# A two-layer transformer kernel: the second layer's queries and keys are projected with features on partitions and brought to the attention layout by DMA alone

## The chip, the cores and the metric

The kernel runs on one core of a Trainium2 chip. The metric is the device time of one execution in microseconds (us). TensorE is written PE, its weight loads PEld, VectorE DVE, ScalarE ACT, GpSimd POOL, and SyncE, which only issues DMAs here, SP.

## The reference

The input x has 2 x 1024 tokens of 256 features. Two layers follow, each of the form x + attention(layernorm(x)) + ffn(layernorm(x)):

```python
xn = _layernorm(x)
x = x + _L0_attn_ref(xn, ...) + _L0_ffn_ref(xn, ...)   # 32 heads of 8, 8 key heads, causal; gelu, float8
xn = _layernorm(x)
x = x + _L1_attn_ref(xn, ...) + _L1_ffn_ref(xn, ...)

def _L1_attn_ref(x, wq, wk, wv, wo, inv_freq):          # 16 heads of 16
    q = apply_rope((x @ wq.T).reshape(b, s, H, HD), inv_freq)
    k = apply_rope((x @ wk.T).reshape(b, s, H, HD), inv_freq)
    v = (x @ wv.T).reshape(b, s, H, HD)
    scores = jnp.einsum('bshd,bstd->bsht', q, k) / jnp.sqrt(jnp.float32(HD))   # over the heads of one token
    weights = jax.nn.softmax(scores, axis=-1)
    attn = jnp.einsum('bsht,bstd->bshd', weights, v)
    return attn.reshape(b, s, HIDDEN) @ wo.T

def apply_rope(x, inv_freq):        # x1, x2 are the even and the odd features of a head
    return jnp.concatenate([x1 * cos - x2 * sin, x1 * sin + x2 * cos], axis=-1)
```

The second layer's attention is within a token: the 16 heads of a token attend to each other. A tile of 128 tokens is therefore 128 little problems of 16 x 16. Eight tokens are put side by side (8 x 16 = 128 rows), and an indicator in 8 more rows of the operands subtracts a huge number where two rows are of different tokens.

## The kernel before

The 2048 tokens are 16 tiles of 128. Every step of the kernel is a stage, a Python function such as `qkv1`, `gT` or `vw`, and `stage.n` is the stage for tile n (or part n of it). Each engine has a list of stages in `ORDER`, written out by hand as one string per engine, and runs them strictly in that order; semaphores alone tie the engines together. So on every engine a stage that waits holds all that stand behind it. SP's list is the order in which nearly all DMAs are issued, and they go through one queue.

PE's heavy work in the first layer is `qk.Q` (scores of one pair of key block and half of the heads, L692) and `pv.Q` (their product with the values, L706), 144 of each, with ACT's `exp.Q` (L958) between them; `up`, `down` are the first feed-forward (L743, L757), `gu` and `dn1` the second (L875, L885). `xnT`, `obT`, `attT`, `o1T`, `at1T` are transposes on PE. Results of PE go to three shared PSUM banks psA, psB, psC in turn; a stage waits until the engine named in `EMPTIED` has taken what stood in its bank.

For tile n of the second layer the stages around the change are:

- `xs.n` (DVE) splits the normalised tile in two float16 parts, `xt.n` (SP, L548) turns them by DMA into xhs, features on partitions.
- `qkv1.2n` (PE, L782) gives queries and keys of 128 tokens by 512 features in six matmuls of 512 columns (xhs stationary), `qkv1.2n+1` the values in six of 256.
- `qk1c.n` (ACT, L991) copies queries and keys out of PSUM. `ro1.n` (DVE, L1400, L1401) and `ro1p.n` (POOL, L1674, L1676) multiply by cos and sin, `ro2.n` (DVE, L1407, L1409) adds and subtracts into rqkv; `v1c.n` (DVE) puts the values there.
- `vw.n` (SP, L501) writes queries, keys and values to qkvscr in HBM, `vr.n` (SP, L509) reads them back in three DMAs, with a row for each head of each of eight tokens and 16 groups side by side, in runs of 64 bytes. For even tiles they land in G, for odd ones in spare halves of w8g and w8l.
- `gT.2n` and `gT.2n+1` (PE, L795) transpose the queries and the keys, four transposes each; `gTq.n` (DVE, L1416) and `gTk.n` (ACT, L1007) copy them to qk1T (odd tiles: in kTf).
- `S1.n` (PE, L828) makes the scores, 16 matmuls with 24 rows, `ex1.n` (ACT, L1016) the exponentials, `PV1.n` (PE, L839), `o1r.n`, `o1T.n`, `o1.n` the outputs, `ow.n` and `at1r.n` (SP, L514, L520) bring them through HBM to one row for each token, `at1T.n`, `wo1.n`, `yo.n`, `yout.n`, `out.n` finish the tile. `hx`, `ht.n` (SP, L556) and `dn1.n` are the feed-forward's end.

At the start `load_first`, `load_constants` and `load_rest` are called ahead of SP's list, with `wt.0`, `wg.0`, `wg.1`, `wt.1` (raw weights) between them. A second pass over all tiles with safer arithmetic exists in the program and isn't taken in these runs.

Of the kernel before, what the change touches and what calls it, by code (L numbers as in the profile page):

```python
# [6 lines left out]
ALU = mybir.AluOpType  # L7
# [181 lines left out]
         "hh": 2, "ge4": 2}  # L189

QUAD_STAGES = {"pe": ("qk", "pv"), "act": ("exp",), "pool": ("mask",)}

# [1576 lines left out]
```

## Time and profile before

| | |
|---|---|
| three runs | 564.24, 564.69, 565.04 us, median 564.69 |
| the profiled execution | 564.45 us, span of its profile 562.7 us |
| PE, ACT, DVE, POOL busy | 518.6, 468.0, 391.0, 234.7 us |
| DMA | 46.05 MB in 214,396 packets |

The span is the time from the first to the last instruction that the profiler saw; 1.75 us of the execution lie outside it. "Busy" is the time in which an engine had at least one instruction running. A row of the grouped view names line, engine, operation, output and inputs, count, then busy time and mean duration of one, then the engine's idle time ahead of them with what ended it.

### The profile page before, as it was taken

To read this page: it belongs to the slowest core of one execution; us is meant where nothing else is said; L and a number is where in the kernel's file an instruction comes from. 1 tells how busy PE (TensorE), PEld (TensorE's weight loads), DVE (VectorE), ACT (ScalarE), POOL (GpSimd) and SP (SyncE) were. 2 spreads that over 40 slices of the span, in tenths; PEclk is the share of its full clock that TensorE was granted. 3 is DMA by queue.
4 is the path that set the end of the run, shared out by engine and by line. 5 is a ranking of instruction groups with operands and counts; after the bars stand their busy time and mean duration, and the time that the engine had idled before them with its cause. 6 is when DMAs were issued, how large, how long until landed. Compare 5 with 4: busy or idle time off the path is not lost.

```text
span 562.7 us, 12411 instructions
## 1 busy us (share of the span) xinstructions
PE 518.6 (92%) x4661; PEld 256.9 (46%) x4705; DVE 391.0 (69%) x845; ACT 468.0 (83%) x607; POOL 234.7 (42%) x302
## 2 busy tenths in 40 slices
...
GB/s 272 284 62 99 57 24 11 73 40 40 47 91 48 103 36 94 62 76 29 77 51 45 128 49 79 85 82 96 75 90 66 53 85 66 68 70 132 125 105 94
DMA packets 214396, 46.05 MB, mean 82 GB/s; under 512 B 197440, under 2 KB 213056, under 8 KB 214336
## 3 DMA queue, kind: packets, MB, share of 16 engines
q1 hardware_dynamic: 213760, 44.93, 40.5%
q8 instruction: 37, 0.61, 0.5%
q10 hardware_dynamic: 576, 0.33, 0.4%
...
## 4 chain that ended last, share of the span: by engine, by line
PE 77%; DMA 6%; DVE 4%; ACT 4%; SPq 3%; issue 3%; POOL 2%; DVEq 0%; ACTq 0%
PE psV L706 23%; PE psS L692 8%; PE psA L875 3%; PE psC L782 3%; PE psS L828 3%; PE psC L875 3%; ACT Pt L958 2%; PE psB L875 2%; PE psB L885 2%; PE psA L885 2%; PE psB L839 2%; PE psA L782 2%; PE psA L743 2%; PE psB L743 2%; PE psC L743 1%
## 5 line engine op out<-in xcount | busy, mean ns | idle before, releaser
L958 ACT ACTIVATE Pt<-psS 128x1024 f32<-128x1024 f32 x288 | 280.1, 1031 | 24.0 <-PE psS L692 19.2
L706 PE MATMUL psV<-Pt,vaug 128*32 128x512 f32 x1152 | 149.8, 605 | 1.8 <-POOL Pt L1633 1.4
L1633 POOL TENSOR_SCALAR_AFFINE_SELECT Pt<-Pt 128x1024 f32<-128x1024 f32 x64 | 71.6, 1143 | 75.7 <-ACT Pt L958 75.5
L692 PE MATMUL psS<-qTf,kTf 32*128 32x512 f16 x576 | 65.8, 388 | 4.8 <-ACT Pt L958 3.1
L692 PEld LDWEIGHTS psS<-qTf,kTf 32*128 32x128 f16 x576 | 17.9, 91 | 84.2 <-ACT Pt L958 51.4
L1683 POOL TENSOR_TENSOR ss<-ss,mhalf 128x1 f32<-128x1 f32 x16 | 9.6, 597 | 87.0 <-DVE ss L1470 87.0
L706 PEld LDWEIGHTS psV<-Pt,vaug 128*32 128x32 f32 x1152 | 25.4, 108 | 42.7 <-issue 34.7
L1016 ACT ACTIVATE stage<-psS 128x1024 f32<-128x1024 f32 x32 | 31.0, 1023 | 7.0 <-PE psS L828 6.9
L1624 POOL TENSOR_TENSOR QXf<-rt,QXf 128x512 f16<-128x512 f32 x16 | 19.9, 1242 | 27.4 <-ACT QXf L945 27.4
L1304 DVE SCALAR_TENSOR_TENSOR gw<-gw,gb 128x512 f32<-128x512 f32 x32 | 27.6, 866 | 4.8 <-ACT gw L973 4.8
L1613 POOL TENSOR_TENSOR rt<-qkv,cs 128x320 f32<-128x320 f32 x16 | 16.1, 1003 | 27.4 <-DVE qkv L1189 19.8
L875 PE MATMUL psA<-wguT,xhs 128*128 128x512 bf16 x97 | 25.4, 380 | 0.9 <-issue 0.5
L1032 ACT ACTIVATE qtmp<-qtmp 128x1024 bf16<-128x1024 f32 x16 | 17.0, 1063 | 10.9 <-DMA stmp<-qtmp 7.8
L1476 DVE SCALAR_TENSOR_TENSOR qtmp<-qtmp,ss 128x1024 f16<-128x1024 f32 x16 | 21.5, 1344 | 6.3 <-ACT qtmp L1037 6.2
L1313 DVE SCALAR_TENSOR_TENSOR ga<-gw,gb 128x512 bf16<-128x512 f32 x32 | 23.0, 718 | 2.0 <-ACT gw L984 2.0
L1674 POOL TENSOR_TENSOR r<-qk,cos 128x256 f32<-128x256 f32 x16 | 13.4, 835 | 25.8 <-ACT qk L991 18.9
L984 ACT ACTIVATE gw<-gw 128x512 f32<-128x512 f32 x32 | 20.8, 651 | 0.0
L1616 POOL TENSOR_TENSOR rt<-qkv,sn 128x160 f32<-128x160 f32 x32 | 20.8, 669 | 0.0
L973 ACT ACTIVATE gw<-gb 128x512 f32<-128x512 bf16 x32 | 20.7, 649 | 0.1
L1455 DVE SCALAR_TENSOR_TENSOR stmp<-stmp,psA 128x512 f32<-128x512 f32 x17 | 11.6, 684 | 12.4 <-ACT stmp L1026 12.2
L1037 ACT ACTIVATE qtmp<-qtmp,ss 128x1024 f16<-128x1024 f32 x16 | 18.5, 1156 | 1.2 <-POOL ss L1683 1.2
L782 PE MATMUL psC<-wqkv,xhs 128*128 128x256 f16 (+1 forms) x102 | 19.1, 324 | 0.0
...
## 6 DMA issues: line engine op xcount, KB each, us to landing
...
```

Of the source, the lines that this page charges most:

```text
L692: e.matmul(psS[j], kd[32 * j:32 * j + k, h, 128 * at:128 * at + 128], qd[32 * j:32 * j + k, 4 * h:4 * h + 4, :].rearrange("p s n -> p (s n ...
L706: ins = e.matmul(psV[32 * j:32 * j + 32, :], vaug[:, at, j, 32 * h:32 * h + 32], Pt[(4 * Q + j) % NP], start=(kb == 0 and h == 0), stop=(k ...
L743: ins = e.matmul(bank[:, 128 * k:128 * k + 128], wt8[:, c, c0:c0 + 128], src[:, c, :], start=(c == 0), stop=(c == 1))
L782: ins = e.matmul(bank[:, 0:c1 - c0], src[:, pt, 128 * a:128 * a + 128], wparts[:, q, a, c0:c1], start=(k == 0), stop=(k == 5))
L875: ins = e.matmul(bank[:], src[:, pt, 128 * c:128 * c + 128], wguT[:, c, c0:c0 + 512], start=(k == 0), stop=(k == 3))
L885: ins = e.matmul(bank[:, 0:256], hT[:, pt, s, :], wpT[:, s, :], start=(k == 0), stop=(k == 15))
L958: e.activation(flat(Pt4[:, u % NP:u % NP + 2, :]), flat(psS4[:, j:j + 2, :]), ACT.Exp, scale=scale).then_inc(S["exp"], 1)
L1016: e.activation(P1[:, 4 * b:4 * b + 8, :].rearrange("p g n -> p (g n)"), flat(psS4[:, b:b + 2, :]), ACT.Exp, scale=SC1).then_inc(S["ex1"], 1)
L1304: e.scalar_tensor_tensor(gw[:, half, :], gw[:, half, :], 1.0 / GA, gb[:, half, :], ALU.add, ALU.mult).then_inc(S["ge1"], 1)
L1313: e.scalar_tensor_tensor(a, gw[:, half, :], 1.0, gg, ALU.add, ALU.mult).then_inc(S["ge3"], 1)
L1476: e.scalar_tensor_tensor(hx_b[:, 1, :], h1, sn[:, 2:3], hx_b[:, 0, :], ALU.mult, ALU.subtract).then_inc(S["hx"], 1)
L1633: e.affine_select(out=p, in_=p, pattern=[[0, 8], [1, 128]], compare_op=ALU.is_ge, fill=0.0, base=0, channel_multiplier=-1).then_inc(S["mas ...
```

## The change

Queries and keys are now projected with features on partitions: the weights are stationary, 128 features at a time, and the 128 tokens move. `qkv1.2n` is 24 matmuls of 128 columns where it was six of 512; the columns of the weights are reordered on the host so that partition p = 16d + h holds feature pair d of head h (`turn`), first all even features, then all odd ones. The tables of cos and sin get the same layout (`turns`, 128 partitions by 1024 tokens); they are made once, by two more activations in `sin.0`, four stages `tT` of four transposes each on PE and five stages `tTc` on ACT. `rab.n` (DVE) multiplies by them straight from PSUM in two instructions of 512 elements, `rr.n` (POOL) adds and subtracts in two of 256, writing the heads that belong to one group side by side. `rw.n` (SP) writes them to rscr in two DMAs, in runs of 8 floats (32 bytes); `rd.n` (SP) reads them in four DMAs of 16 partitions, in runs of 512 bytes, right to where `gTq` and `gTk` had put them. The stages `gT`, `gTq`, `gTk`, `qk1c`, `ro1`, `ro1p`, `ro2` are gone from the first pass. The values alone go through vscr (`vw.n`, one DMA of 128 KB in runs of 64 bytes; `vr.n`, one where there were three), and `at1r.n` reads runs of 64 bytes where it read rows of 1 KB. The first loads become stages in SP's list, two raw weights (`wgx`) and the later tiles of x (`lx`) are issued by ACT, and the casts `w8` no longer wait for a buffer between the second and the third. All lists in `ORDER` are written anew, so every stage may stand elsewhere.

```diff
+                    if part == 0:
+                        for c in range(4):
+                            for k, (pt, q, a) in enumerate(((0, 0, 0), (1, 0, 0), (0, 1, 0), (0, 0, 1), (1, 0, 1), (0, 1, 1))):
+                                ins = e.matmul(bank[:, 128 * c:128 * c + 128], wparts[:, q, a, 128 * c:128 * c + 128],
+                                               src[:, pt, 128 * a:128 * a + 128], start=(k == 0), stop=(k == 5))
+                        ins.then_inc(S["qkv1"], 1)
+                        return
...
+            def tT(m):
...
+                    ins = e.transpose(bank[:, 128 * k:128 * k + 128], turns[:, 1 + m // 2, c0:c0 + 128], identf[:])
...
+            def rab(n):
...
+                w.wait_ge("qkv1", 2 * n + 1)
+                w.wait_ge("rr", 2 * n)
+                for k in range(2):
+                    e.tensor_tensor(r1[:, k, :].rearrange("p (e s t) -> p e s t", e=2, s=2), bank,
+                                    turns[:, k:k + 2, t0:t0 + 128].unsqueeze(2).to_broadcast([128, 2, 2, 128]),
+                                    ALU.mult).then_inc(S["rab"], 1)
...
+            def rr(n):
+                dst = flat(rqkv[n % 2][:, 0:2, :])
+                w.wait_ge("rab", 2 * n + 2)
+                w.wait_ge(f"d_rw{n % 2}", 32 * (n // 2))
+                for f, op in enumerate((ALU.subtract, ALU.add)):
+                    e.tensor_tensor(dst[:, 256 * f:256 * f + 256].rearrange("p (b s j a) -> p s b j a", b=4, s=2, j=4),
+                                    by_group(r1[:, f, 0:256]), by_group(r1[:, f, 256:512]), op).then_inc(S["rr"], 1)
...
+            def rw(n):
+                src = flat(rqkv[n % 2][:, 0:2, :]).rearrange("p (f m a) -> p f m a", f=2, a=8)
+                dst = rscr[n].rearrange("b s j (f i) (h a) -> f (i h) (b s j) a", f=2, a=8)
+                for f in range(2):
+                    w.wait_ge("rr", 2 * n + f + 1)
+                    e.dma_start(dst[f], src[:, f, :, :]).then_inc(S[f"d_rw{n % 2}"], 16)
+
+            def rd(n):
+                w.wait_ge(f"d_rw{n % 2}", 32 * (n // 2 + 1))
...
+                w.wait_ge("S1", 4 * (n - 1))
+                for b in range(4):
+                    dst = (qk1Todd if odd(n) else qk1T)[32 * b:32 * b + 16, :, :, :].rearrange("p s j n -> p (s j) n")
+                    e.dma_start(dst, rscr[n, b].rearrange("s j d n -> d (s j) n")).then_inc(S[f"d_rd{n % 2}"], 16)
...
+                e.activation(turns[:, 2, :].rearrange("p (m h) -> p m h", h=16),
+                             ang[:, 0, :].unsqueeze(2).to_broadcast([128, 64, 16]), ACT.Sin)
...
-    "gT": lambda m: ("gTk" if m % 2 else "gTq", m // 2 + 1), "gTagain": lambda n: ("gTm", n - NT + 1),
+    "gT": lambda m: ("gTk" if m % 2 else "gTq", m // 2 - NT + 1), "gTagain": lambda n: ("gTm", n - NT + 1),
```

On PE, from the scores of tile 5 to those of tile 6, this stood in a row before (L795 are the transposes gT, L828 the scores S1, L839 is PV1, L692 qk, L706 pv, L743 up, L875 gu, L610 and L611 xnT):

```order
L828 MATMUL psS<-kTf 128x128 x16
L706 MATMUL psV<-Pt,vaug 32x512 x8
L795 MATMUL psB<-identf,G 128x128 x4
L692 MATMUL psS<-qTf,kTf 128x512 x4
L610 MATMUL psC<-identf,xn 128x128
L611 MATMUL psC<-identf,xn 128x128
L875 MATMUL psA<-wguT,xhs 128x512 x4
L839 MATMUL psB<-stage,w8l 32x128 x16
L692 MATMUL psS<-qTf,kTf 128x512 x4
L743 MATMUL psC<-x8T,w8g 128x128 x8
L795 MATMUL psA<-identf,G 128x128 x4
```

And at the same place now (L842 is the new projection, L903 S1, L764 pv, L801 up, L950 gu, L750 qk, L914 PV1, L785 and L786 wo0):

```order
L842 MATMUL psC<-xhs,wqkv 128x128 x24
L785 MATMUL psA<-wo,attT 128x256
L786 MATMUL psA<-wo,attT 128x256
L903 MATMUL psS<-kTf 128x128 x16
L764 MATMUL psV<-Pt,vaug 32x512 x4
L801 MATMUL psB<-x8T,big 128x128 x8
L950 MATMUL psC<-wguT,xhs 128x512 x4
L750 MATMUL psS<-qTf,kTf 128x512 x4
L950 MATMUL psA<-wguT,xhs 128x512 x4
L764 MATMUL psV<-Pt,vaug 32x512 x4
L750 MATMUL psS<-qTf,kTf 128x512 x4
L764 MATMUL psV<-Pt,vaug 32x512 x4
```

The groups of four transposes are gone from between the first layer's work, and nothing takes their place.

On SP, near the end, from ow.11 on, the list before (L514 ow, L520 at1r, L525 out, L509 vr, L556 ht, L548 xt, L501 vw):

```order
L514 DMA oscr<-o_0 128x16x16
L520 DMA at_0<-oscr 128x256
L525 DMA out<-yout 128x256
L509 DMA w8g<-qkvscr 128x16x16 x2
L509 DMA w8l<-qkvscr 128x16x16
L556 DMA_TRANSPOSE stmp<-qtmp 128x16x128
L548 DMA_TRANSPOSE xhs<-xn1T 128x4x128
L501 DMA qkvscr<-rqkv 128x3x256
L514 DMA oscr<-o_0 128x16x16
L509 DMA G<-qkvscr 128x16x16 x3
```

The list now, from ow.11 on (L573 ow, L565 rd, L579 at1r, L587 out, L557 rw, L524 vw, L618 ht, L610 xt, L537 vr):

```order
L573 DMA o2scr<-o_0 128x256
L565 DMA kTf<-rscr 16x8x128 x4
L579 DMA at_0<-o2scr 128x16x16
L587 DMA out<-yout 128x256
L557 DMA rscr<-rqkv 128x32x8 x2
L524 DMA vscr<-rqkv 128x16x16
L618 DMA_TRANSPOSE stmp<-qtmp 128x16x128
L610 DMA_TRANSPOSE xhs<-xn1T 128x4x128
L537 DMA G3v<-vscr 128x16x16
L573 DMA o2scr<-o_0 128x256
L565 DMA qk1T<-rscr 16x8x128 x4
```

The writes and reads of queries and keys, six issues, stand between the steps of the last tiles; xt.15 comes behind rw.14 and vw.14.

On ACT, at the start, the list before ran tc.0 (L931, L932), qh.0 (L945), sin.0 (L924, L925), wh.0 (L995), g.0 (L966), qh.1 and then exp.0 (L958):

```order
L931 ACT_TABLE_LOAD
L931 ACTIVATE qtmp<-r 128x1024
L932 ACTIVATE qtmp<-r 128x1024
L945 ACTIVATE QXf<-rt 128x32x16
L924 ACT_TABLE_LOAD
L924 ACTIVATE sin<-ang 128x64
L925 ACTIVATE cos<-ang,hpi 128x64
L995 ACTIVATE wqkv<-stmp 128x1536
L966 ACTIVATE gb<-psC 128x512
L945 ACTIVATE QXf<-rt 128x32x16
L958 ACT_TABLE_LOAD
L958 ACTIVATE Pt<-psS 128x1024 x2
```

The list now, from wh.0 on (L1094 wh, L1061 sq, L1019 and L1020 tc, L1033 qh, L1046 exp, L1007 to L1012 sin):

```order
L1094 ACTIVATE wqkv<-stmp 128x1536
L1061 ACTIVATE gw<-gb 128x512
L1019 ACTIVATE qtmp<-r 128x1024
L1020 ACTIVATE qtmp<-r 128x1024
L1033 ACTIVATE QXf<-rt 128x32x16
L1046 ACTIVATE Pt<-psS 128x1024 x4
L1007 ACT_TABLE_LOAD
L1007 ACTIVATE sin<-ang 128x64
L1008 ACTIVATE cos<-ang,hpi 128x64
L1010 ACTIVATE big<-ang 128x1024
L1012 ACTIVATE big<-ang,hpi 128x1024
L1046 ACT_TABLE_LOAD
```

sin.0 now stands behind exp.0 and exp.1, with a table load on either side, and has two new activations of 1024 elements. Ahead of the rows shown, ACT now runs qh.0, g.0, sq.0, fh.0, g.1, fh.1 and th.0; with the sq.1 shown (L1061), six stages of the feed-forward have moved ahead of exp.0.

## Rows read from the trace of the kernel before

**Rows 1.** The page: busy time of each engine, share of the span

```profile
PE 518.6 (92%) x4661; PEld 256.9 (46%) x4705; DVE 391.0 (69%) x845; ACT 468.0 (83%) x607; POOL 234.7 (42%) x302
```

**Rows 2.** Windows: length, PE, PEld, DVE, ACT, POOL busy, clock, DMA share, GB/s

```profile
0.00:20.00 20.00, 5.84 (x16) 2.91 (x16) 13.26 (x38) 3.91 (x4) 5.99 (x19) 1.00 0.94 301
...
40.00:80.00 40.00, 35.04 (x286) 13.82 (x284) 31.27 (x62) 38.72 (x53) 27.65 (x32) 1.00 0.21 55
80.00:120.00 40.00, 36.85 (x283) 15.66 (x285) 35.20 (x72) 38.50 (x53) 22.29 (x28) 1.00 0.22 52
...
160.00:200.00 40.00, 39.74 (x402) 20.69 (x406) 28.09 (x64) 38.81 (x55) 17.42 (x24) 1.00 0.45 72
...
360.00:400.00 40.00, 39.63 (x411) 21.67 (x407) 24.69 (x54) 34.94 (x44) 13.65 (x18) 1.00 0.59 109
...
500.00:520.00 20.00, 17.67 (x188) 11.65 (x189) 14.93 (x35) 7.78 (x11) 4.87 (x8) 1.00 0.59 108
520.00:540.00 20.00, 16.54 (x206) 12.02 (x207) 12.65 (x26) 8.76 (x12) 1.94 (x4) 1.00 0.80 124
540.00:563.00 23.00, 16.23 (x136) 10.55 (x135) 12.30 (x34) 6.07 (x8) 1.04 (x2) 0.85 0.42 93
```

**Rows 3.** The timeline of PE from 404 us: start, duration of the group

```profile
404.75 0.66 PE L795 MATMUL psA<-identf,w8g 128*128 128x128 f32 x4
405.25 0.60 PE L715 MATMUL psB<-identf,ob 128*128 128x128 f32 x4
405.68 1.46 PE L782 MATMUL psC<-wqkv,xhs 128*128 128x512 f16 x6
407.07 0.39 PE L692 MATMUL psS<-qTf,kTf 32*128 32x512 f16 x4
407.40 0.62 PE L743 MATMUL psA<-x8T,w8g 128*128 128x128 fp8e4 x8
407.86 0.61 PE L743 MATMUL psB<-x8T,w8g 128*128 128x128 fp8e4 x8
```

**Rows 4.** Groups by line, shapes apart: busy us, mean ns | idle before

```profile
L782 PEld LDWEIGHTS psC<-wqkv,xhs 128*128 128x128 f16 x102 | 9.2, 98 | 7.4 <-issue 3.0
...
L1674 POOL TENSOR_TENSOR r<-qk,cos 128x256 f32<-128x256 f32 x16 | 13.4, 835 | 25.8 <-ACT qk L991 18.9 <-DVE rqkv L1409 5.8 <-issue 0.9
...
L1464 DVE SCALAR_TENSOR_TENSOR qtmp<-stmp,psA 128x512 f32<-128x512 f32 x10 | 6.8, 682 | 1.7 <-PE psA L875 1.5
...
L991 ACT ACTIVATE qk<-psC 128x512 f32<-128x512 f32 x8 | 4.9, 608 | 1.1 <-PE psC L782 1.1
...
L931 ACT ACTIVATE qtmp<-r 128x1024 bf16<-128x1024 f32 x3 | 3.2, 1074 | 6.6 <-DMA r<-in_wgu 6.2 <-DVE wguT L1150 0.4
```

**Rows 5.** DMA queues, the whole span: packets, MB, share of 16 engines

```profile
q1 hardware_dynamic: 213760, 44.93, 40.5%
```

**Rows 6.** DMA queues from 505 to 508.5 us, where ow.11 writes alone

```profile
q1 hardware_dynamic: 2064, 0.13, 36.5%
```

**Rows 7.** DMA queues from 491.8 to 496.3 us, where vr.12 reads

```profile
q1 hardware_dynamic: 6226, 0.41, 91.8%
```

**Rows 8.** The timeline of SP from 480 us: start and duration of each issue

```profile
504.65 0.36 SPq L514 DMA_DIRECT2D oscr<-o  x1
509.38 0.33 SPq L520 DMA_DIRECT2D at<-oscr  x1
...
515.95 1.19 SPq L548 DMA_TRANSPOSE xhs<-xn1T  x1
...
547.95 0.36 SPq L514 DMA_DIRECT2D oscr<-o  x1
```

**Rows 9.** The chain that ended last, from 0 to 45 us

```profile
19.92 5.71 DMA stage<-in_wg
...
28.20 1.28 ACT L958
29.49 1.94 ACT Pt L958 x2
```

More of the change, by code:

```diff
@@ L225 @@
     "wo0": lambda n: ("xa", n + 1), "up": lambda m: ("fh" if m % 2 else "g", m // 2 + 1), "down": lambda n: ("yff", n + 1), "flagT": lambda n: ("flag", 1), "wsum": lambda m: ("wmin", m + 1),
-    "xn1T": lambda n: ("xn1f", n - NT + 1), "qkv1": lambda m: ("v1c" if m % 2 else "qk1c", m // 2 + 1),
-    "gT": lambda m: ("gTk" if m % 2 else "gTq", m // 2 + 1), "gTagain": lambda n: ("gTm", n - NT + 1),
+    "xn1T": lambda n: ("xn1f", n - NT + 1), "qkv1": lambda m: ("v1c", m // 2 + 1) if m % 2 else ("rab", m + 2) if m < 2 * NT else ("qk1c", m // 2 - NT + 1),
+    "tT": lambda m: ("tTc", m + 1),
+    "gT": lambda m: ("gTk" if m % 2 else "gTq", m // 2 - NT + 1), "gTagain": lambda n: ("gTm", n - NT + 1),
     "PV1": lambda n: ("o1r", n + 1),
@@ L257 @@
 idc vz tab cst w8 w8m w8s tsc tm tcs tw ln0 xn xnTc qkvc va wide q0 kl xs fTc rmax rcomb mxn mTc ob att attTc xa ge1 ge3 ge3b a8c yff
-wh wsq wsum ln1 xn1 xn1Tc xn1f wl wmin v1c ro1 ro2 gTq m1 gTm o1r o1 sg hh ssm hx at1Tc yo yout osum flag rng rngb
+wh wsq wsum ln1 xn1 xn1Tc xn1f wl wmin v1c tT tTc rab rr gTq m1 gTm o1r o1 sg hh ssm hx at1Tc yo yout osum flag rng rngb
 zero gz zf rs0 rope ql mask ge4 xf rs1 ro1p rsg w8a""".split()
@@ L562, in all_landed @@
                     w.wait_ge(f"d_vw{p}", 16 * 8 * passes)
-                w.wait_ge("d_vr", 48 * NT * passes)
+                for p in range(2):
+                    w.wait_ge(f"d_vr{p}", read_back(NT * passes - 2 + p))
+                    w.wait_ge(f"d_rd{p}", 128 + 64 * 8)
                 w.wait_ge("d_ow", 16 * NT * passes)
@@ L809, in S1m @@
             def S1m(n):
-                w.wait_ge("gTq", n + 1)
-                w.wait_ge("gTk", n + 1)
+                w.wait_ge("gTq", n - NT + 1)
+                w.wait_ge("gTk", n - NT + 1)
                 for j in range(4):
@@ L818, in S1m @@
                             ins.then_inc(S["S1m"], 1)
+            def tT(m):
+                w.wait_ge("sin", 1)
+                w.wait_ge("d_id", 16)
+                bank = shared("tT", m)
+                for k in range(4):
+                    c0 = 512 * (m % 2) + 128 * k
+                    ins = e.transpose(bank[:, 128 * k:128 * k + 128], turns[:, 1 + m // 2, c0:c0 + 128], identf[:])
+                ins.then_inc(S["tT"], 1)
             def S1(n):
-                k = 24 if n < NT else 25
-                w.wait_ge("gTq", n + 1)
-                w.wait_ge("gTk", n + 1)
+                if n < NT:
+                    w.wait_ge(f"d_rd{n % 2}", 128 + 64 * (n // 2 + 1))
+                w.wait_ge("gTq", n - NT + 1)
+                w.wait_ge("gTk", n - NT + 1)
                 w.wait_ge("gTm", n - NT + 1)
@@ L987, in qk1c, with tTc @@
                 w.wait_ge("qkv1", 2 * n + 1)
-                w.wait_ge("ro1p", 2 * (n + 1 - len(qk1)))
-                w.wait_ge("ro1", 2 * (n + 1 - len(qk1)))
+                w.wait_ge("ro1p", 2 * (n - NT))
+                w.wait_ge("rab", 2 * n)
                 bank = psM[filled["qkv1", 2 * n] % len(psM)]
-                e.activation(qk1[n % len(qk1)][:], bank[:], ACT.Copy, scale=1.0 / WUP if n < NT else 1.0).then_inc(S["qk1c"], 1)
+                e.activation(qk1[0], bank[:], ACT.Copy).then_inc(S["qk1c"], 1)
+            def tTc(m):
+                if m == 4:
+                    w.wait_ge("tT", 4)
+                    w.wait_ge("tTc", 2)
+                    e.activation(turns[:, 2, :], turns[:, 0, :], ACT.Copy).then_inc(S["tTc"], 1)
+                    return
+                bank = psM[filled["tT", m] % len(psM)]
+                w.wait_ge("tT", m + 1)
+                e.activation(turns[:, m // 2, 512 * (m % 2):512 * (m % 2) + 512], bank[:], ACT.Copy,
+                             scale=1.0 / WUP).then_inc(S["tTc"], 1)
             def wh(n):
@@ L1037, in hxa @@
                 e.activation(hx_b[:, 0, :], h1, ACT.Copy, scale=ss[n % len(ss)][:, 2:3]).then_inc(S["hxa"], 1)
-            run = {"wh": wh, "wsq": wsq, "qh": qh, "g": g, "hxa": hxa, "sin": sin, "tc": tc, "tde": tde, "exp": exp, "sq": sq, "fh": fh, "th": th, "qk1c": qk1c, "gTk": gTk, "ex1": ex1,
+            run = {"tTc": tTc, "wgx": wgx, "lx": lx, "wh": wh, "wsq": wsq, "qh": qh, "g": g, "hxa": hxa, "sin": sin, "tc": tc, "tde": tde, "exp": exp, "sq": sq, "fh": fh, "th": th, "qk1c": qk1c, "gTk": gTk, "ex1": ex1,
                    "tg": tg, "ssq": ssq}
@@ L1387, in v1c @@
                                 ALU.mult).then_inc(S["v1c"], 1)
-            def half1(k, s):
-                return r1[:, k, 256 * s:256 * s + 256].rearrange("p (h d) -> p h d", d=8)
-            def ro1(n):
-                src = qk1[n % len(qk1)][:].rearrange("p (h d e) -> p h d e", d=8, e=2)
-                cb = cos1[:, n % NB, :].unsqueeze(1).to_broadcast([128, 32, 8])
-                sbb = sin1[:, n % NB, :].unsqueeze(1).to_broadcast([128, 32, 8])
-                w.wait_ge("sin", 1)
-                w.wait_ge("tc", 12)
-                w.wait_ge("qk1c", n + 1)
-                w.wait_ge("ro2", 2 * n)
-                e.tensor_tensor(half1(1, 0), src[:, :, :, 0], sbb, ALU.mult).then_inc(S["ro1"], 1)
-                e.tensor_tensor(half1(1, 1), src[:, :, :, 1], cb, ALU.mult).then_inc(S["ro1"], 1)
+            def rab(n):
+                bank = psM[filled["qkv1", 2 * n] % len(psM)][:].rearrange("p (e s t) -> p e s t", e=2, s=2)
+                t0 = 128 * (n % NB)
+                w.wait_ge("tTc", 5)
+                w.wait_ge("tc", 12)
+                w.wait_ge("qkv1", 2 * n + 1)
[4 more added lines that the diff above has]
+                                    ALU.mult).then_inc(S["rab"], 1)
```

243 lines of the change are left out of this document (145 added, 98 removed), and 238 rows, old and new, of the table ORDER.

## The prediction

> **What bounds the kernel now.** First the page: PE is busy 518.6 of 562.7 us, ACT 468.0, DVE 391.0 [rows 1]. A mean over the span doesn't say where a microsecond of PE is worth one, so I read the windows next [rows 2]. They show three stretches. Up to about 120 us ACT is the fuller engine: 38.7 of 40 us and 38.5 of 40, with PE at 35.0 and 36.9. From 160 us PE is at 39.7 of 40 with ACT at 38.8, and by 360 us PE stands alone, 39.6 against 34.9. From 500 us on nothing is full: PE has 17.7 of 20, 16.5 of 20 and 16.2 of 23, while DMA has a share of 0.59 and then 0.80. So there is an ACT stretch, a long PE stretch and a tail of latencies through HBM. Each edit is priced by the stretch in which it lies.
>
> The chain that ended last says the same of the two ends. At the start it goes through loads, 5.7 us for the last raw weights among them, and the first exponential runs at 29.5 us [rows 9]. In the tail SP's timeline shows ow.11 issued at 504.65, at1r.11, which waits for its landing, at 509.38, and xt.15 at 515.95 [rows 8]. I call 504.65 the start of the tail; from there to the span's end are 58.05 us.
>
> **The transposes go.** Four transposes gT take 0.50 us of PE from their start to the next group's (404.75 to 405.25) [rows 3]. A group itself lasts 0.66, and where the next isn't ready part of its end shows too; I take 0.55, between 0.50 and 0.60. Of 32 such groups 26 (tiles 0 to 12) stand ahead of the tail: 14.3 us, with bounds of 13.0 and 15.6. Those of tiles 0 to 4 lie where ACT is nearly as full as PE, so they count only if ACT loses as much. It does: qk1c and gTk are gone, 0.61 us each [rows 4], 1.2 a tile against 1.1 on PE. The six groups in the tail stand where PE idles: 0.
>
> **The projection.** Six matmuls of 512 columns take 1.39 us (405.68 to 407.07). The new one has 24 of 128 columns, each with its own weights. `up` is the same pattern in another type, eight matmuls of 128 columns in 0.46 us (407.40 to 407.86), 57.5 ns each [rows 3]; 24 make 1.38 us, so this costs nothing. Below that it can't go, since the columns are the same number. The upper bound is a weight load that nothing hides: 98 ns each, the mean of the float16 loads of this very projection [rows 4], 24 of them 2.35 us, 0.96 more a tile, 14.4 us for the 15 tiles projected before the tail's middle. I take 0, because `up` also shows loads of 98 ns and keeps the pace of 57.5. The Trainium skill has a rule against this edit: TensorE: Matmul & The Clock Gate, Back-to-back issue gap, gives about 81 ns for each matmul in a sustained stream of loads and matmuls of 128 columns. By that the projection is 1.94 us and the kernel some 8 us slower than by the row; the trace of `up` does not agree with it.
>
> **The rotation.** DVE gives up six instructions (ro1, ro2, gTq) and gets two of 512 elements from PSUM, nearest row 0.68 us each; POOL keeps two of 256 elements, 0.84 [rows 4]. DVE is at 25 to 35 us of 40 all through the middle [rows 2], so its gain is hidden. What is new is that rab reads PSUM itself: the shared bank is held until DVE comes to it, for 1.4 us where ACT took 0.61. PE's other stages need that bank third next; I allow 0 to 4 us and put it with the waits below.
>
> **The start.** ACT's list, in the ACT stretch: four tTc of 512 elements and one of 1024, 3.5 us; two sines of 1024, 2.1; a further table load, 1.28 as ahead of exp.0 [rows 9]: 6.9 us more (1024 elements by L931, 1.07, 512 by L991 [rows 4]). Against it stand qk1c.0 and qk1c.1 (1.2) and six stages of 0.62 us moved ahead of exp.0, where ACT waited for loads (3.8). The loads: the three raw weights that were queued behind constants and x are issued at once on two queues, and the cast of the third no longer waits. But the transposes qt.0 and kt.0 still queue behind some 6 MB, which at the 301 GB/s of the first 20 us [rows 2] takes, with what is issued late, until about 24 us, so the first exponential comes at 26 to 28 us where it was 29.5; I take 2 us of gain. The sum is -0.1: nothing, with bounds of -4 and +4. The four tT on PE, 2.0 us, fall in the ACT stretch, where PE has 3 to 5 us of slack in 40 [rows 2]: 0, at most 2.
>
> **DMA.** Runs set its time. ow.11 alone: 2064 packets in 36.5% of 16 engines over 3.5 us, 9.9 ns a packet of 64 bytes written; vr.12: 6226 in 91.8% over 4.5 us, 10.6 ns a packet read [rows 6, 7]. For a tile, rw writes 8192 packets of 32 bytes. No row has them; between nothing less than half a packet of 64 (5 ns) and the whole queue's mean, 40.5% of 16 x 562.7 over 213,760, 17 ns [rows 5], I take 10, since the 64-byte row is nearest: 5.1 us. rd (512 packets) is about 1 us, at1r has 2048 packets for 128, 0.9 us more, vr loses two of three DMAs of 2048, 2.6 us less. So a tile has some 4.3 us more of DMA, and the queue's share goes from 0.41 to about 0.53. The Trainium skill, DMA: Bandwidth & Descriptors, Specifications, says that transfers under 512 bytes are read-modify-write. Here 64-byte writes cost no more than 64-byte reads; 32-byte ones are not in the trace.
>
> **The middle's latency.** From qkv1 to S1 the new path needs 1.4 + 1.4 (rab) + 1.7 (rr) + 7.5 (rw: 5.1 and the fixed part of a lone DMA, for which I take 2.4: ow.11 took 4.7 [rows 8] with 1.4 of transfer, others less) + 4 (rd) = 16 us. Counting PE's stages between the two in the new list at the durations above, tiles 0 to 12 have 24 to 66 us. That covers it with some queueing. But from 340 to 400 us four to five tiles rotate, where DMA has 0.59 of 40 us already [rows 2]; 4.3 each takes it to about 0.95. I add 1 us of stalls for it and for the banks, bounds 0 and 9.
>
> **The tail.** Set T = 0 at ow.11. at1r.11 lands at 8 instead of 6.8 (its own 2048 packets). dn1.11 and ht.12 follow, then xt.15, behind rw.14 and vw.14 on the queue: landed at about 17.5, where before it was issued at 11.3 (515.95). Then rab, rr, rw.15 (issued at 23, landed at 31), rd.15 (36), vr.15 (41, since SP issues it last), PV1.15, ow.15 at 43.5 instead of 43.3 (547.95) [rows 8], at1r.15 1.3 longer, and the rest as before: 59.5 instead of 58.05. The tail's transposes and copies that are gone pay for most of the longer writes. I take +1.5, bounds -2 and +8.
>
> **The sum** is made against the profiled execution: 562.7 - 14.3 + 0 - 0.1 + 1 + 1.5 = 550.8 of span, and 1.75 outside it: 552.5 us. That execution took 564.45, the median of three is 564.69, so the two count as one. What this measurement can tell from no change is about 0.2%, 1.1 us.
>
> **The rivals.**
>
> *DMA takes the middle too (0.15).* If the queue's load between 340 and 400 us and SP's strict order make kt, qt and xt late, qk waits and the whole list with it. For it speaks the share of 0.95, against it the gaps of 24 us and more. It gives back 5 to 12 us: 558 to 564, by its bounds some of it not faster.
>
> *Short writes cost much more (0.10): slower.* Each ns above 10 for a packet of 32 bytes adds 0.5 us a tile. On the path are the last three tiles and the cluster of five at 340 to 400 us, some 8 tiles, 4 us for each ns once the queue is full. It decides from 13 ns on; at 17, the mean packet, it takes 16 us: 568; at 20, 578. For it speaks that a write of 32 bytes is less than anything that the kernel writes now; against it that 64-byte packets show no cost by bytes at all.
>
> *Loads of weights are not hidden (0.07).* At 98 ns the term is 14.4 us: 567. At the skill page's 81 it is 8 us: 560.5. `up` speaks against both.
>
> *The start gains more (0.12).* If the first exponential comes at 24 us and the new order fills the 8 us in which PE idles between 40 and 120 us, 4 to 9 us more go: 544 to 548.
>
> The forecast itself has 0.56, with a range of its own of 548 to 557. The range over all cases is 543 to 566. Faster: the forecast, the better start and two thirds of the first rival and a third of the third, 0.80; within 0.2%: 0.06; slower: 0.14.
>
> **What the new profile should show.** No rows for gT; the projection at 1.35 to 1.45 us from its start to the next group's; about 21,500 packets a tile in q1 and a share of 0.50 to 0.56; PE above 39 of 40 us from 160 us on; ow.11 issued near 490; first exponential at 26 to 28 us. A q1 share above 0.65 means dear short writes. PE at 37 or less of 40 in the middle with waits of qk on kTf or qTf means the first rival. I am wrong if PE's idle time outside the two ends grows by more than 10 us.

## The result, and the profile after

The changed kernel takes 573.69 us (median of four, 571.2 to 574.46) beside 564.87 for the kernel before on the same chip: a ratio of 1.0159, 95% interval 1.0142 to 1.0176. It is 9 us slower where 12 us less was forecast. The profiled execution took 574.46 us.

The page of the changed kernel, against [rows 1, 5]: busy times, the queue, and of its DMA table the row of rw (median us from issue to landing at the end):

```profile
span 572.7 us, 12792 instructions
PE 521.6 (91%) x4881; PEld 262.4 (46%) x4881; DVE 375.2 (66%) x794; ACT 457.7 (80%) x582; POOL 245.9 (43%) x299
...
q1 hardware_dynamic: 313408, 42.50, 50.1%
...
rscr<-rqkv SPq DMA_DIRECT2D x32, 128.0 KB, 6.5
```

Its windows, with the columns of [rows 2]:

```profile
160.00:200.00 40.00, 38.16 (x404) 19.86 (x397) 25.97 (x56) 35.35 (x48) 16.57 (x20) 0.96 0.66 62
...
320.00:360.00 40.00, 37.01 (x432) 20.27 (x428) 26.88 (x58) 31.69 (x39) 23.83 (x29) 1.00 0.78 76
360.00:400.00 40.00, 37.17 (x392) 20.53 (x392) 18.33 (x40) 30.30 (x38) 12.51 (x16) 0.91 0.55 78
500.00:520.00 20.00, 17.12 (x195) 11.26 (x194) 12.73 (x27) 7.97 (x11) 8.33 (x11) 0.94 0.65 78
520.00:540.00 20.00, 16.41 (x213) 12.06 (x215) 10.11 (x21) 6.77 (x8) 2.64 (x3) 0.89 0.80 102
```

From 320 to 400 us PE has lost nearly 6 of 80 us, and its clock is 0.91 behind 360 us. The window of before that [rows 2] doesn't show:

```profile
320.00:360.00 40.00, 39.64 (x412) 19.85 (x413) 28.80 (x64) 35.77 (x47) 19.75 (x26) 1.00 0.41 67
```

Where the loss comes from is seen in PE's timeline. The first two rows are a projection and what starts behind it, then the start of `qk.96`, the stall, and `qk.102`:

```profile
327.75 1.50 PE L842 MATMUL psC<-xhs,wqkv 128*128 128x128 f16 x24
329.19 0.40 PE L750 MATMUL psS<-qTf,kTf 32*128 32x512 f16 x4
...
346.74 0.49 PE L750 MATMUL psS<-qTf,kTf 32*128 32x512 f16 x4
...
362.83 0.48 PE L668 MATMUL psB<-identf,at 128*128 128x128 f32 x1 [5.82 <-DMA at<-o2scr]
...
376.78 0.64 PE L750 MATMUL psS<-qTf,kTf 32*128 32x512 f16 x4
```

The 24 matmuls take 1.44 us to the next group's start, as forecast. The same two `qk` groups before the change:

```profile
348.70 0.52 PE L692 MATMUL psS<-qTf,kTf 32*128 32x512 f16 x4
...
372.08 0.48 PE L692 MATMUL psS<-qTf,kTf 32*128 32x512 f16 x4
```

At `qk.96` the new kernel is 2.0 us ahead, and six steps later it is 4.7 behind. One wait of 5.82 us lies between, in at1T.5, for the landing of at1r.5. Behind it PE works at the lower of its two clocks (1.2 GHz; the granted clock is 0.50 from 362.8 to 366.3 us). SP's timeline tells why that is late (a row with x4 is four issues):

```profile
341.50 0.55 SPq L537 DMA_DIRECT2D G3v<-vscr  x1
342.42 10.06 SPq L557 DMA_DIRECT2D rscr<-rqkv  x4
352.52 3.38 SPq L573 DMA_DIRECT2D o2scr<-o  x1
356.01 1.27 SPq L602 DMA_TRANSPOSE qTf<-QXf  x1
358.76 0.38 SPq L579 DMA_DIRECT2D at<-o2scr  x1
359.24 2.66 SPq L565 DMA_DIRECT2D kTf<-rscr  x4
```

Issuing is itself held up. The four issues of rw.7 and rw.8 keep SP for 10.06 us, ow.5 stands behind them and needs 3.38 instead of some 0.4, its data land 6.23 us after its start, and only then can at1r.5 be issued. The tail shows the same thing, against [rows 8]:

```profile
510.17 0.43 SPq L573 DMA_DIRECT2D o2scr<-o  x1
...
515.13 2.64 SPq L557 DMA_DIRECT2D rscr<-rqkv  x2
517.81 3.36 SPq L524 DMA_DIRECT2D vscr<-rqkv  x1
521.28 3.15 SPq L618 DMA_TRANSPOSE stmp<-qtmp  x1
524.54 1.20 SPq L610 DMA_TRANSPOSE xhs<-xn1T  x1
```

ow.11 is issued at 510.17, not near 490, and rw.14, vw.14 and ht.12 hold xt.15 until 524.54, though its input was ready at 518.95 (DVE's last write of xn1T).

### The profile page after: what moved, and what is told of

Its sections match the earlier page's. It is cut to its first block, busy times and chain, and to the rows that moved or that the text cites. A ratio compares the mean times of both kernels' runs of the same rounds, so it can differ in the third digit from the quotient of the medians.

```text
span 572.7 us, 12792 instructions
## 1 busy us (share of the span) xinstructions
PE 521.6 (91%) x4881; PEld 262.4 (46%) x4881; DVE 375.2 (66%) x794; ACT 457.7 (80%) x582; POOL 245.9 (43%) x299
## 4 chain that ended last, share of the span: by engine, by line
PE 63%; DMA 10%; SPq 10%; ACT 6%; DVE 5%; issue 3%; POOL 3%; DVEq 0%; POOLq 0%; ACTq 0%
PE psV L764 18%; PE psS L750 7%; ACT Pt L1046 3%; SPq L557 3%; DMA rscr<-rqkv 3%; PE psB L950 3%; PE psC L950 2%; PE psA L960 2%; PE psS L903 2%; SPq L565 2%; DMA kTf<-rscr 2%; PE psA L950 2%; PE psA L801 2%; DMA stage<-in_wg 1%; POOL rqkv L1782 1%
## 5 line engine op out<-in xcount | busy, mean ns | idle before, releaser
L1046 ACT ACTIVATE Pt<-psS 128x1024 f32<-128x1024 f32 x288 | 279.5, 1030 | 35.8 <-PE psS L750 30.8
L764 PE MATMUL psV<-Pt,vaug 128*32 128x512 f32 x1152 | 153.2, 614 | 1.2 <-POOL Pt L1736 1.1
L750 PE MATMUL psS<-qTf,kTf 32*128 32x512 f16 x576 | 66.6, 391 | 8.7 <-ACT Pt L1046 4.0
L750 PEld LDWEIGHTS psS<-qTf,kTf 32*128 32x128 f16 x576 | 17.9, 91 | 86.0 <-ACT Pt L1046 44.1
L1114 ACT ACTIVATE stage<-psS 128x1024 f32<-128x1024 f32 x32 | 31.0, 1024 | 23.0 <-PE psS L903 23.0
L1782 POOL TENSOR_TENSOR rqkv<-r 128x256 f32<-128x256 f32 x32 | 37.1, 1184 | 24.0 <-DVE r L1494 24.0
L764 PEld LDWEIGHTS psV<-Pt,vaug 128*32 128x32 f32 x1152 | 25.0, 109 | 41.3 <-issue 35.4
L1578 DVE SCALAR_TENSOR_TENSOR qtmp<-qtmp,ss 128x1024 f16<-128x1024 f32 x16 | 22.8, 1423 | 6.4 <-ACT qtmp L1135 6.3
L950 PE MATMUL psB<-wguT,xhs 128*128 128x512 bf16 x92 | 23.7, 380 | 0.0
L950 PE MATMUL psA<-wguT,xhs 128*128 128x512 bf16 x84 | 22.5, 392 | 0.0
L950 PE MATMUL psC<-wguT,xhs 128*128 128x512 bf16 x80 | 20.6, 380 | 0.0
L1061 ACT ACTIVATE gw<-gb 128x512 f32<-128x512 bf16 x32 | 20.5, 645 | 0.1
```

Source lines behind the costliest of these rows:

```text
L750: e.matmul(psS[j], kd[32 * j:32 * j + k, h, 128 * at:128 * at + 128], qd[32 * j:32 * j + k, 4 * h:4 * h + 4, :].rearrange("p s n -> p (s n ...
L764: ins = e.matmul(psV[32 * j:32 * j + 32, :], vaug[:, at, j, 32 * h:32 * h + 32], Pt[(4 * Q + j) % NP], start=(kb == 0 and h == 0), stop=(k ...
L950: ins = e.matmul(bank[:], src[:, pt, 128 * c:128 * c + 128], wguT[:, c, c0:c0 + 512], start=(k == 0), stop=(k == 3))
L1046: e.activation(flat(Pt4[:, u % NP:u % NP + 2, :]), flat(psS4[:, j:j + 2, :]), ACT.Exp, scale=scale).then_inc(S["exp"], 1)
L1061: e.activation(gw[:, half, :], gb[:, half, :], ACT.Square).then_inc(S["sq"], 1)
L1114: e.activation(P1[:, 4 * b:4 * b + 8, :].rearrange("p g n -> p (g n)"), flat(psS4[:, b:b + 2, :]), ACT.Exp, scale=SC1).then_inc(S["ex1"], 1)
```

## The experiments

**One entry of SP's list moved.** rw.8 goes behind at1r.5:

```diff
- rw.7 rw.8 ow.5 qt.13 at1r.5 rd.7 vr.7
+ rw.7 ow.5 qt.13 at1r.5 rw.8 rd.7 vr.7
```

> The changed kernel with one entry of SP's list moved: rw.8, the write of tile 8's queries and keys, goes from ahead of ow.5 to behind at1r.5. Theory (SP's queue in its fixed order): the 5.8 us wait of TensorE at 362.83 us is ow.5 held behind the four blocked issues of rw.7 and rw.8, 10.06 us long; without rw.8's two issues ow.5 goes out about 5 to 6.5 us earlier, the wait falls to under 1 us, the clock is not dropped behind it, and the time falls by 6 to 8 us, to about 566 to 568. Rival (the transfers themselves are the bound, the DMA engines being full of short packets in this stretch): ow.5 lands no earlier than before or the wait comes back at S1 of tile 8, whose rd.8 is later, and the time falls by less than 2 us.

573.25 us, ratio to before 1.0150 (1.0130 to 1.0169): hardly anything, which is the rival's number. SP and PE there:

```profile
350.46 0.34 SPq L573 DMA_DIRECT2D o2scr<-o  x1
...
353.09 0.38 SPq L579 DMA_DIRECT2D at<-o2scr  x1
353.52 4.27 SPq L557 DMA_DIRECT2D rscr<-rqkv  x2
357.89 4.47 SPq L565 DMA_DIRECT2D kTf<-rscr  x4
```

```profile
365.03 1.24 PE L903 MATMUL psS<-kTf 24*128 24x128 f32 x16 [4.57 <-DMA kTf<-rscr]
```

The wait for at1r.5 is gone as the theory has it, but rw.8 now stood ahead of rd.7, and S1.7 waits 4.57 us for that. The move cured one victim and made another. It didn't decide between the theories.

**Long runs.** rw writes the same bytes in rows of 1 KB; the scratch then holds them in another layout, so the second layer's scores are of other features.

```diff
- dst = rscr[n].rearrange("b s j (f i) (h a) -> f (i h) (b s j) a", f=2, a=8)
+ dst = rscr[n].rearrange("b s j d n -> (b s j d n)").rearrange("(f p c) -> f p c", f=2, p=128)
```

> The changed kernel with rw's 256 KB a tile written in rows of 1 KB instead of runs of 32 bytes; everything else, the order included, stays. The scratch then holds the numbers in another layout, so the scores of the second layer are formed from other features and the output is not the reference's. Theory (the price of the short runs is the issues that block SP, not the DMA engines' time): rw's issues fall from 2 to 3.4 us to below 0.5 us each, the wait at 362.83 us falls to under 1 us, the tail's ow.11 goes out nearer 495 us, and the time falls by 10 to 14 us, to 560 to 564. Rival A (the order of the list is the price whatever the packets are): the time falls by less than 4 us. Rival B (the short packets also slow every other transfer): queue q1's share falls from 50.1% by more than 8 points and the time falls by more than 14 us, below 560.

553.85 us, ratio 0.9814 (0.9795 to 0.9832): 11 us below the kernel before and some 20 below the changed one. Page and windows:

```profile
q1 hardware_dynamic: 186432, 42.50, 38.7%
...
rscr<-rqkv SPq DMA_DIRECT2D x32, 128.0 KB, 1.8
```

```profile
320.00:360.00 40.00, 39.79 (x454) 21.50 (x454) 26.52 (x59) 33.95 (x43) 21.84 (x26) 1.00 0.54 99
360.00:400.00 40.00, 39.79 (x417) 20.88 (x412) 20.95 (x46) 35.26 (x45) 15.94 (x20) 1.00 0.55 81
```

Nothing else of the change was touched, so the length of the runs is what turned the gain into a loss. Rival A is out. The share falls by 11.4 points and the time by more than 14 us, which are rival B's numbers: there is more to the short runs than the issues that I had seen blocked. From the starts of the `qk` groups the 21.6 us of span split in 3.0 at 182 us (S1.1 waiting for rd.1), 8.0 between `qk.96` and `qk.102`, 0.9 behind that, and 9.8 from `qk.138` to the end (87.95 us against 78.19; before the change 82.84). Of the 8.0 us PE idles for 5.7, and for 2.3 it takes longer over the same stages, at a mean granted clock of 0.89 where the long runs have 1.00.

**rng.0 behind at1Tc.15** on DVE:

```diff
- yo.14 hx.15 rng.0 at1Tc.15
+ yo.14 hx.15 at1Tc.15 rng.0
```

> The changed kernel with rng.0, the first of the final sampling steps, moved on VectorE behind at1Tc.15, the last copy that the last output projection waits for. Theory: rng.0 lies on the chain of the end (561.54 to 563.69 us), and the time falls by 1.5 to 2.4 us. Rival: the transfer of the last at tile bounds the copy, rng.0 only fills a wait, and the time changes by less than 0.5 us.

575.16 us, 1.0191 (1.0171 to 1.0211): not faster. wo1.15 starts 1.2 us earlier (0.6 of that is there at wo1.14 already), but then the flag's transposition waits 2.16 us for rng, and the last group starts at 566.32 instead of 565.41. rng.0 is on the end's path on either side of the copy.

**The suspected cost alone, in the kernel before.** Ahead of each vw.n, SP writes 256 KB of the same tile to a scratch that nobody reads, in 8192 runs of 32 bytes; and as a control the same bytes by the same two issues in rows of 1 KB.

```diff
+ def xw(n):
+     w.wait_ge("ro2", 2 * n + 2)
+     for f in range(2):
+         e.dma_start(dst[f], src[:, f, :, :]).then_inc(S[f"d_xw{n % 2}"], 16)
```

> The kernel before with one thing added: ahead of each of its sixteen vw.n SP also writes 256 KB from the same tile to a scratch that nobody reads, in 8192 runs of 32 bytes, by two issues, as rw does in the changed kernel. Nothing else of the change is in. Theory (blocked issues of short runs in SP's fixed order cost time by themselves): queue q1's share rises by 8 to 11 points, each added pair holds SP 2.5 to 6 us, and the kernel gets 5 to 15 us slower, to 570 to 580, mostly at waits for ow and at1r that follow an added pair and in the tail. Rival (the cost is in the changed kernel's own order or in its rd reads, which this kernel has not): below 3 us slower.

> The control to the extra short runs: the kernel before with the same added 256 KB a tile, by the same two issues at the same places of SP's list, but in rows of 1 KB (256 packets a tile). With short runs it took 73 us more. Theory (the short packets are the price): under 8 us more than before. Rival (any two issues and 256 KB more at that place cost as much): over 30 us more.

Short: 637.84 us, 1.1313 (1.1283 to 1.1342), 73 us more. Long: 568.29 us, 1.0079 (1.0060 to 1.0099), 4.4 more. SP around one such pair, first with the short runs (then vw, at1r):

```profile
190.58 2.50 SPq L510 DMA_DIRECT2D xscr<-rqkv  x2
193.13 3.35 SPq L503 DMA_DIRECT2D qkvscr<-rqkv  x1
196.52 1.15 SPq L529 DMA_DIRECT2D at<-oscr  x1
```

and with the long ones:

```profile
181.93 0.82 SPq L510 DMA_DIRECT2D xscr<-rqkv  x2
182.79 0.45 SPq L503 DMA_DIRECT2D qkvscr<-rqkv  x1
183.28 0.53 SPq L529 DMA_DIRECT2D at<-oscr  x1
```

The pair holds SP for 2.5 us, and the next write is held for 3.35 more. vw now lands after 6.5 us (median) where it took 2.7. PE then waits in many places: 5.18 and 5.17 us for at at 200 and 405 us, 4.28 and 5.37 for G at 150 and 481. Of the 73 us PE idles for 48, and for 25 it takes longer over the same work (busy 543.7 us where it was 518.6), at a mean granted clock of 0.93 where it was 0.98. I had expected 5 to 15 us and was far too low. The reason is probably that a list that was laid out for vw landing in 2.7 us has no room for 4 more anywhere; no run shows that by itself. The changed kernel, with lists laid out anew, pays 20 us instead of 73.

**Half of each rw from another queue.** ScalarE issues the second half, at the place of its list where the addition is done; bytes, runs and DMA engines stay.

```diff
  def rw(n):                            # SP
-     for f in range(2):
-         w.wait_ge("rr", 2 * n + f + 1)
-         e.dma_start(dst[f], src[:, f, :, :])...
+     w.wait_ge("rr", 2 * n + 1)
+     e.dma_start(dst[0], src[:, 0, :, :])...
+ def rwa(n):                           # ACT
+     w.wait_ge("rr", 2 * n + 2)
+     e.dma_start(dst[1], src[:, 1, :, :])...
```

> The changed kernel with the second of rw's two issues (features 8 to 15 of every head, 4096 runs of 32 bytes) taken from SP and given to ScalarE's queue, behind the addition that makes it; the bytes, the runs and the 16 DMA engines stay the same, and SP keeps the first issue, which took 0.36 to 0.44 us where it was not held up. Theory A (the price of the short runs is SP's blocked second issue and what queues up behind it): SP's part of each rw falls from 2.5 to 3.5 us to about 0.5 us, the wait at 362.83 us shrinks to under 1.5 us and the tail loses about 5 us, so the time falls by 10 to 16 us, to 558 to 564. Theory B (the transfers are the price: the engines are full of 8192 short packets whoever issues them, and rd or ow lands late anyway): less than 4 us is won. ScalarE pays for its issues too: if they block it for 2 us each, it gets slower than the changed kernel.

566.54 us, 1.0053 (1.0029 to 1.0078): about 6 us less than the changed kernel by the ratios, between the two theories. ScalarE's timeline, then SP's and PE's in the tail:

```profile
338.58 0.41 ACTq L1009 DMA_DIRECT2D rscr<-rqkv  x1
...
339.87 4.33 ACTq L1009 DMA_DIRECT2D rscr<-rqkv  x1
```

```profile
500.51 3.62 SPq L588 DMA_DIRECT2D out<-yout  x1
504.17 0.54 SPq L574 DMA_DIRECT2D o2scr<-o  x1
```

```profile
512.59 0.48 PE L669 MATMUL psB<-identf,at 128*128 128x128 f32 x1 [4.54 <-DMA at<-o2scr]
```

A lone issue of 4096 short packets takes 0.36 to 0.58 us on either queue; the one that follows 1.3 us after another is held for 4.33 us. So it is what is still outstanding on the issuer's own queue that holds it: SP's issue for rw.8, at 338.5 us right behind that for rw.7, is held for 3.15 us, and ScalarE's first, 0.1 us later, takes 0.41. ScalarE pays for being held: its next exponential starts at 344.30 us, 2.57 after the end of the one before, and PE waits 1.34 us for it. The wait at 182 us is gone and the one at 363 us is 1.74 us. But in the tail out.9 is held all the same, ow.11 goes out at 504.17 us where the long runs have 496.26, and it lands after 5.4 us where they take 1.7. The DMA share is 1.01 from 500 to 520 us. With two queues the packets' times overlap (the share is 1.11 from 320 to 360 us), so this number doesn't say how full the 16 engines are.

**The same with xt.15 ahead of ht.12.**

> The kernel with half of rw on ScalarE's queue, and xt.15 ahead of ht.12 in SP's list. In the changed kernel xn1T of tile 15 was ready at 518.95 us and xt.15 was issued at 524.54, behind vw.14 and ht.12; the projection of tile 15 waited 3.26 us for it. Theory (SP's order in the tail costs by itself): 1.5 to 3 us less than with half of rw on ScalarE alone. Rival (once the issues no longer block, the order is no matter): within 1 us of it.

567.44 us, 1.0060 (1.0039 to 1.0082): the rival. PE's wait for xhs (0.81 us) is gone, and the one of S1.14 grows from 0.73 to 2.00 us.

**The lists bent round the short runs**, half of rw still on ScalarE's queue:

```diff
- rw.7 rw.8 ow.5 qt.13 at1r.5 rd.7 vr.7
+ rw.7 ow.5 qt.13 at1r.5 rd.7 vr.7 rw.8
...
- out.9 ow.11 rd.13 at1r.11
+ ow.11 at1r.11 out.9 rd.13
```

> Short runs kept, half of each rw on ScalarE's queue, and the lists bent round them: rw.8 behind rd.7 and vr.7 on both queues, ow.11 and at1r.11 ahead of out.9, xt.15 ahead of ht.12, rd.15 ahead of ht.13, the second half of rw.14 later on ScalarE. Theory (most of what was left, 12 us against long runs, is bad places in the order): 558 to 563 us. Rival (the engines' time for 8192 short packets is what is left, whatever the order): less than 3 us below the kernel with half on ScalarE's queue, 564 to 568.

563.19 us, 0.9947 (0.9927 to 0.9967): by the ratios 6 us less than with half of rw on ScalarE alone. That is the theory's side, at the edge of its range. The profiled execution was one of 567.39. Windows:

```profile
320.00:360.00 40.00, 40.00 (x464) 21.78 (x462) 27.34 (x62) 33.96 (x43) 21.91 (x26) 1.00 0.75 92
360.00:400.00 40.00, 40.00 (x407) 20.18 (x405) 20.95 (x46) 35.27 (x45) 15.09 (x19) 1.00 0.63 87
...
500.00:520.00 20.00, 14.03 (x169) 10.53 (x166) 9.33 (x22) 5.87 (x8) 1.62 (x4) 0.83 1.01 115
```

This parts the cost. In the middle the DMA engines carry the short packets at a share of 0.75 and PE is full: `qk.96` to `qk.102` takes 22.04 us as with long runs, and at `qk.138` the short packets have cost 1.3 us where they cost 11.9. So there the price was the held issues and their places in the list. In the tail no order that I tried helped: from `qk.138` to the end it takes 91.4 us in this execution, at a granted clock of 0.83 from 500 to 540 us. A median execution is 4.2 us shorter, and no trace says where.

**Long runs that end in the layout the second layer needs, first form.** The tokens of a group are put side by side on the way into PSUM, rw writes runs of 256 bytes, and S1 reads its operands at a stride of eight numbers:

```diff
- return turned(n, s)[32 * b:32 * b + 24, j, :]
+ return tile[32 * b:32 * b + 24, :].rearrange("p (n m) -> p m n", m=8)[:, 4 * s + j, :]
```

> A version meant to keep the changed kernel's gain without its short runs, with the right output: the eight tokens of a group are put next to each other on the way (the transposition into PSUM of the rotation tables and the projection write their columns in that order), so that a partition's row for one block is 256 contiguous bytes. rw then writes 1024 runs of 256 bytes a tile instead of 8192 of 32, rd reads 64 rows of 4 KB, and S1 takes its two operands from the tile at a stride of eight numbers instead of one. Order, issues and bytes stay. Theory (the runs' length is the price, 19 us of it): 552 to 557 us, 8 to 12 us below the kernel before. Rival A (S1's operands at a stride cost TensorE: 512 matmuls and their loads, 10 to 20 ns more each): 5 to 10 us more than that, 558 to 566. Rival B (writing PSUM in runs of 16 bytes slows the projection or the rotation behind it): the projection's six matmuls of a quarter take more than 0.38 us.

568.18 us, 1.0052 (1.0033 to 1.0072). Rival B is out, since the projection takes 1.34 to 1.45 us as in the changed kernel. It is rival A, and more than it: groups of S1's weight loads and matmuls here, then the same in the kernel with rows of 1 KB, where the operands are contiguous:

```profile
L908 PEld LDWEIGHTS psS<-kTf 24*128 24x128 f32 x256 | 16.1, 327 | 4.0 <-issue 2.5 <-DMA kTf<-rscr 1.4
L908 PE MATMUL psS<-kTf 24*128 24x128 f32 x256 | 18.4, 435 | 1.0 <-DMA kTf<-rscr 1.0
```

```profile
L903 PEld LDWEIGHTS psS<-kTf 24*128 24x128 f32 x256 | 8.0, 186 | 4.4 <-issue 2.5 <-DMA kTf<-rscr 1.8
L903 PE MATMUL psS<-kTf 24*128 24x128 f32 x256 | 9.5, 283 | 1.4 <-DMA kTf<-rscr 1.4
```

S1 takes 2.28 us a tile instead of 1.17, 17.7 us over sixteen; the distance to the 553.85 of long runs is 14.3. From 120 to 540 us no wait of PE is longer than 0.6 us.

**Second form.** The rotation writes as in the changed kernel, rw in runs of 256 bytes, S1 reads the queries in runs of eight, and DVE copies the keys once to where they stand in a row:

```diff
+ def k1(n):
+     w.wait_ge(f"d_rd{n % 2}", 128 + 64 * (n // 2 + 1))
+     w.wait_ge("S1", 4 * n)
+     for i in range(2):
+         e.tensor_copy(k1c[i].rearrange("p j (h a) -> p j h a", a=8), by_m(n)[:, 4 + 2 * i:6 + 2 * i, :, :])...
```

> Long runs again, and the output is the reference's, but without the stride of eight that made S1 slow: the rotation writes its tile as in the changed kernel, rw writes 1024 runs of 256 bytes a tile, rd reads 64 rows of 4 KB with queries and keys of a head side by side, S1 reads the queries in runs of eight numbers as its moving operand, and VectorE copies the keys once (two copies of 128x256 a tile) into a tile where they stand one after another for the weight load. Theory (run length is the price; eight numbers in a row are read at full speed; the copies of some 0.4 us each are hidden in VectorE's slack of a third): S1 takes 1.2 us a tile again and the kernel 553 to 559 us, 6 to 11 us below the kernel before. Rival (the copy sits on the way from rd to S1 and stands in VectorE's fixed order): 560 to 566. If S1 takes 1.7 us a tile, the moving operand alone is slowed by its runs.

558.64 us, 0.9875 (0.9855 to 0.9896): 7 us below the kernel before, 16 below the changed one by the ratios. S1 takes about 1.1 us again, and PE is full in the middle:

```profile
534.06 0.73 PE L910 MATMUL psS<-kTf 24*128 24x128 f32 x16 [1.97 <-DVE ang L1542]
534.61 0.62 PE L910 MATMUL psS<-kTf,ang 24*128 24x128 f32 x16
```

```profile
320.00:360.00 40.00, 40.00 (x472) 22.14 (x472) 29.57 (x67) 34.06 (x43) 24.07 (x29) 1.00 0.56 92
```

The copy costs waits of 1.2 to 2.0 us at four of the sixteen S1, two ahead of 240 us and two in the tail, the last above.

## Why the prediction was wrong

**What held.** The projection's 24 matmuls take 1.34 to 1.45 us, 56 to 60 ns each (but for the last tile, 2.25 us at the lower clock); 57.5 was the term. The Trainium skill's 81 ns (TensorE: Matmul & The Clock Gate, Back-to-back issue gap) is not what this trace shows. The first exponential comes at 26.5 us, first `qk` 2.4 us earlier, 2 was the term. The packet's price held too: the queue's busy time differs by (0.501 x 572.7 - 0.387 x 551.1) x 16 = 1178 us between short and long runs, for 126,976 packets, 9.3 ns a packet; with the rows of 1 KB that stand in their place it is a little more, near the 10 that I took. In the records the 32-byte packets themselves last 8.1 ns in the mean; the others last longer beside them (those of 64 bytes 11.8 ns, with long runs 10.1). A read-modify-write below 512 bytes, which the Trainium skill states (DMA: Bandwidth & Descriptors, Specifications), doesn't show in a packet's time here. The share is 0.501, the bottom of the range given, 3.7 us a tile and not 4.3. One reason is a term that the text left out: ow now writes rows of 1 KB, so a tile has 19,588 packets and not 21,500. So the rival "short writes cost much more", which was to decide from 13 ns a packet on, is not what happened. (By its own 4 us for each ns, 20 ns would make 580, not 578.)

**What held by luck.** Take the short runs out and the measured 553.85 stands beside the forecast 552.5, but two errors cancel in that. With long runs ow.11 goes out at 496.3 us, 8.4 us earlier than before the change, where transposes and start together were put at 14.4 and ow.11 "near 490". And from there to the end it takes 54.9 us, 3.2 less than before, where 1.5 more was forecast. The transposes themselves were priced rightly: from `qk.42` to PV1.11 the 23 groups that stood there took 11.8 us, 0.51 each. But this stretch is only 7.1 us shorter. One group of pv and one of PV1 more stand in it now, 1.9 us; the other 2.8 are spread over the groups that stayed, and their cause is open. Up to `qk.42` no more than the start's gain is there (1.6 us at `qk.0`, 1.2 at `qk.42`).

**The step that failed** is "The middle's latency". It added up the path from qkv1 to S1, found 16 us against gaps of 24 to 66, and took 1 us of stalls. (One term of the path was too low: POOL's two instructions take 1.18 us each where 0.84 was taken.) At 182 us the path itself was late: S1.1 waited for rd.1, 3.0 us of the price. But nothing on it was late at 363 us, where most was lost. What was late is ow.5, which has nothing to do with it and stands behind rw.7 and rw.8 in SP's list. The text priced rw as 5.1 us of the engines and never as time of the queue that issues it: 2.5 us and more for a pair, 10.06 for two, and up to 3.4 for the plain DMA right behind it. Measured, the term is 11.9 us (3.0 + 8.0 + 0.9) where 1 was taken and 9 was the bound. Over the whole stretch the DMA queue was not full. The text feared a share of 0.95 between 340 and 400 us, for which it took the 0.59 of the window from 360 us for all 60 us; measured are 0.78 up to 360 us and 0.55 behind. The rival "DMA takes the middle too" named SP's strict order and PE at 37 of 40, which is what the windows show; it looked for the waits at kTf and qTf and gave 5 to 12 us back, which for the middle is right. The sign named for being wrong, 10 us more of idle PE outside the ends, didn't come: from 120 us to ow.11 PE idles 8.9 us where it was 3.5. Part of the loss is work at the lower clock, which isn't idle time.

**The tail's term** was mis-sized: +1.5, bounds -2 and +8. From ow.11 to the end the changed kernel takes 62.5 us where 59.5 was worked out, with 58.05 before and 54.9 with long runs: +4.5, of which the short runs make +7.7 and the rest of the change -3.2. Another 2.1 us of the short runs' price lie between `qk.138` and ow.11. The chain worked out was nearly right up to the transfers of tile 15: counted from ow.11, rw.15 landed at 32.2 us (31 forecast) and vr.15 at 42.0 (41). Then ow.15 was issued at 47.6 where 43.5 stood. That left 2.5 us from vr.15's landing to ow.15, and from PV1.15's start to ow.15 alone it takes 3.5 (3.4 before). And PE came to PV1.15 only at 44.1, behind dn1.13 and two groups of gu that the text left out, in part at the lower clock.

Together, ahead of ow.11 the forecast was -13.4 us (-14.3 - 0.1 + 1) and the measured change +5.5: -8.4 without the short runs, and 11.9 + 2.1 for them. From ow.11 on it was +1.5 and is +4.5.

**What stays open.** Of the 9.8 us that the short runs cost from `qk.138` on, PE idles for about 5.5, and for about 4.2 it takes longer over the same stages, at a lower granted clock (0.89 from 520 to 540 us against 0.94 with long runs). How the idle part divides between held issues and engines that are shared is not shown: splitting the issues over two queues and reordering them didn't bring the end nearer, but no run takes the held issues away and keeps everything else.
